# A new order of the image step in a vision transformer layer with routed experts

## The chip, the cores and the metric

The kernel runs on one core of a Trainium2 chip. The metric is the time of one execution on the device in microseconds (us). "Before" was timed three times; the profile is of one more execution.

## What is computed

The reference is one transformer layer over 16 images of 128 tokens and 256 channels, all in float32:

```python
h = tok(x)                                   # x: (16, 4, 128, 256); softmax over 4 groups, weighted sum
h = h + attn(layernorm(h))                   # 16 heads of 16, relative position bias, softmax over 128 keys
h = h + moe(layernorm(h))                    # 8 experts 256 -> 1024 -> 256, the best two of each token
```

`tok` weighs four groups per channel, with weights from a small two-layer network. `moe` keeps the two largest gates of a token and sums the two experts' outputs, weighted.

## The kernel before

The program is written by hand for each engine. Every engine works through its own list in order, and semaphores (`wait_ge`, `then_inc`) hold an instruction until another engine has finished.

**Image stage.** Each engine has a function `step(i, u, ...)`, called for i = 0 to 16. A step treats three images at a time, one pipeline stage apart: image i in front (`front`), i - 1 (`back`), i - 2 (`late`), with the preparation of i + 1 (`nxt`). What one step holds, by engine:

- TensorE (PE): `project_qk(i)` (L786) and `project_v(i)` (L797), 16 and 4 matmuls; `scores(i, 0)` and `scores(i, 1)` (L809), each for eight heads into the two banks `psS`, so that the second needs the first half's `biased` to be done; `context(i-1, c)` (L819), c = 0 to 3, transposes four heads' probabilities into `psP`; `values(i-1, w)` (L833) multiplies them with the values; `out_project(i-2)` (L844); `spread_sums`, `turn_x(i+1)` (L767), `turn_xn2(i-2)` (L859) are transposes; `gate_logits(i-2)` (L865); in steps 7, 11 and 14 also `ranks`.
- ScalarE (ACT): `exp(b, u, c)` (L592), four heads each, with row sums; `qk_evac` (L573), `pT_evac` (L581), `r_evac` (L567), `x1T_evac` (L561), `x2T_evac` (L609) and `v_evac` (L602) copy results of PE out of PSUM; `first_group(i+2)` (L553) starts the token mixing of a later image.
- VectorE (DVE): `select_groups(i+1)` (L1106) ends the token mixing, with the statistics of the first norm; `mask_keys(i, 0)` (L267); `residual(i-2)` (L1155), which waits for `project_v(i)` since both use the bank `psVO`, with the statistics of the second norm; `reciprocals` (L1136) and `spread` (L1140); `first_norm`, `second_norm` (L1093); `biased(i, c)` (L1126), c = 0 to 3, adds the position bias to four heads' scores and finds the minimum that `exp(i, u, c)` needs; `normalise` (L1149); `keep_logits` (L1167). In gate steps (6, 10, 13) also the gates of a batch of images, and in rank steps (7, 11, 14) `rows` (L1219 to L1226), which turns ranks into record positions.
- GpSimd (POOL): the power -1/2 of both norms (L434), `mask_keys(i, 1)`, and `scatter_records` (L445), an indirect DMA for each image and choice. From the second pair on, a pair waits for the landing of the pair before (`scat`). Batch 2 (images 8 to 10) goes out as two pairs in step 14 and one in step 15.
- SyncE (SP) issues the plain DMAs in order: in each step the stores of `xn2` and `h`, in every second step a load of 1 MB of W2 (L318), then, behind the tile table that DVE makes after step 14 (L1302 to L1323), the first load of W1 (L330), and behind the landing of all records of images 0 to 10 the records' reload (L323, L336).

**Expert stage.** 39 tiles of 128 token slots; each is gathered from DRAM (L482), transposed (L935), multiplied with W1 (L947) and W2 (L959), and scattered with addition (L491). The first 14 tiles use only images 0 to 10.

Of the kernel before, what the change touches and what calls it, by code (L numbers as in the profile page):

```python
# [63 lines left out]
def vit_layer_kernel(nc, x, tok_w1, tok_b1, tok_w2, tok_b2, Wq, Wk, Wv, Wo, rel_emb,  # L64
# [8 lines left out]
    with ExitStack() as ctx:  # L73
# [442 lines left out]
        def _(act):  # L516
# [39 lines left out]
            def x1T_evac(b):  # L556

                act.wait_ge(x1T_ps, b + 1)
                if later(b):
                    act.wait_ge(v_ps, b)  # L560
                act.copy(x1T[:, :], psQK[:, DC * S:2 * DC * S]).then_inc(x1T_sb, 1)  # L561
# [13 lines left out]
            def pT_evac(b, c):  # L575
                act.wait_ge(pT_ps, NCH * b + c + 1)
                if isinstance(b, int) and b == 0 and c < 2:
                    pass
                else:
                    act.wait_ge(pv_ps, NCH * b + c - 1)  # L580
                act.copy(pT[c % 2][:, :], psP[c % 2][:, :]).then_inc(pT_sb, 1)  # L581

            def exp(b, u, c):
                act.wait_ge(s_min, NCH * b + c + 1)
                if c == 0 and later(b, 1):
                    act.wait_ge(s_rcp, b - 1)
                own_wait(act)
                for n in range(CH):
                    h = c * CH + n
                    k = HEADS * (u % 2) + h  # L590
                    blk = prob[u % 2][:, h * S:(h + 1) * S]
                    i = act.activation(blk, blk, ACT.Exp, bias=smin[:, k:k + 1], scale=-1.0,  # L592
                                       accum_out=ssum[:, k:k + 1])
                i.then_inc(s_exp, 1)
# [14 lines left out]
                act.copy(x2T[:, :], psG[:, 0:DC * S]).then_inc(x2T_sb, 1)  # L609

            def step(i, u, front=True, back=True, late=True, nxt=True, batch=None, tanh=False, ahead=True):
                if back:
                    exp(i - 1, 1 - u, 2)
                if front:
                    qk_evac(i)
                if back:
                    pT_evac(i - 1, 0)
                    pT_evac(i - 1, 1)
                    exp(i - 1, 1 - u, 3)
                if tanh:  # L620
                    select_tanh(1, NG - 1)
                if batch is not None:
                    gate_exps(batch)
                if back:
                    pT_evac(i - 1, 2)
                    pT_evac(i - 1, 3)
                if back:
                    r_evac(i - 1)
                if ahead:
                    first_group(i + 2)  # L630
                if front:
                    exp(i, u, 0)
                if late:
                    x2T_evac(i - 2)
                if nxt:
                    x1T_evac(i + 1)
                if front:
                    exp(i, u, 1)
                    v_evac(i)

            def gate_exps(g):
                act.wait_ge(gate_exp_in, g + 1)
                n = BATCHES[g][1]
                act.activation(second_e[:, 0:n], below[:, 0:n], ACT.Exp).then_inc(gate_exp, 1)
# [59 lines left out]
        def _(pe):  # L704
# [8 lines left out]
            for g in range(G):  # L713
                i = pe.transpose(psVO[:, g * P:(g + 1) * P], tok_w2_wide[:, g * P:(g + 1) * P], ident[:, :])
# [56 lines left out]
            def spread_sums(b):  # L771

                pe.wait_ge(s_wide, b + 1)
                for c in range(DC):
                    i = pe.transpose(psCX[:, (DC + c) * S:(DC + c + 1) * S],
                                     srcw[:, c * P:(c + 1) * P], ident[:, :])
                i.then_inc(r_ps, 1)
# [91 lines left out]
            def ranks(g, last):  # L869

                pe.wait_ge(gate_step, GATE_N * g + MASKS_AT)
                pe.wait_ge(lg_sb, last)
                n = BATCHES[g][1]
                pe.matmul(psG[:, RKC:RKC + (n + 1) * E], ones[:, :], counts[:, 0:(n + 1) * E], start=True, stop=False)
                for k in range(1, n + 1):
                    pe.matmul(psG[:, RKC + k * E:RKC + (n + 1) * E], ones[:, :], counts[:, 0:(n + 1 - k) * E],
                              start=False, stop=False)
                pe.matmul(psG[:, RKC:RKC + n * E], before[:, :], counts[:, E:(n + 1) * E],
                          start=False, stop=True).then_inc(rank_ps, 1)

            def step(i, u, front=True, back=True, late=True, nxt=True, batch=None, sums=False, select=False):

                if front:
                    project_qk(i)
                if back:
                    context(i - 1, 1 - u, 0)
                    context(i - 1, 1 - u, 1)
                if late:
                    out_project(i - 2)
                if front:  # L890
                    project_v(i)
                if sums:
                    image_sums(2, 1)
                if batch is not None:
                    ranks(batch, i - 2)
                if back:
                    values(i - 1, 0)
                    context(i - 1, 1 - u, 2)
                if front:
                    scores(i, 0)  # L900
                if back:
                    context(i - 1, 1 - u, 3)
                    spread_sums(i - 1)
                if late:
                    turn_xn2(i - 2, batch)
                if nxt:
                    turn_x(i + 1)
                if back:
                    values(i - 1, 1)
                if front:  # L910
                    scores(i, 1)
                if select:
                    pe.wait_ge(x2T_sb, i - 1)
                    select_logits(1, NG, B)
                if late:
                    gate_logits(i - 2)
# [85 lines left out]
        def _(dve):  # L1002
# [93 lines left out]
            def select_groups(b, done=None):  # L1096

                dve.wait_ge(tok_first, b + 1)
                for g in range(1, G):
                    if g == 2 and done is not None:  # L1100
                        top_two(*done)
                    if g == 3 and done is not None:
                        top_index(*done)
                    if g > 1:
                        dve.wait_ge(tok_acc, (G - 1) * b + g - 1)
                    dve.scalar_tensor_tensor(out=hcol(b), in0=xw2[:, bass.ds(b * (G * D) + g * D, D)],  # L1106
                                             scalar=tsel[:, bass.ds(b + g * B, 1)], in1=hcol(b),
                                             op0=ALU.mult, op1=ALU.add).then_inc(tok_acc, 1)
                dve.wait_ge(tok_acc, (G - 1) * (b + 1))
                norm_stats(0, hcol(b), ln1, LN1_N * b)  # L1110

# [116 lines left out]
            def step(i, u, front=True, back=True, late=True, nxt=True, done=None, gate=None, place=None, hidden=False):  # L1228

                if nxt:  # L1230
                    select_groups(i + 1, done)
                elif done is not None:
                    top_two(*done)
                    top_index(*done)
                if gate is not None:
                    gate_inputs(gate)
                if front:
                    mask_keys(dve, i, 0)
                if late:
                    residual(i - 2)  # L1240
                if back:
                    reciprocals(i - 1, 1 - u)
                    spread(i - 1)
                if nxt:
                    first_norm(i + 1)
                if place is not None:
                    rows(place)
                if late:
                    second_norm(i - 2)
                if gate is not None:  # L1250
                    masks(gate)
                if front:
                    biased(i, u, 0)
                    biased(i, u, 1)
                if hidden:
                    hidden_end(1, NG - 1)
                if gate is not None:
                    gates(gate)
                if back:
                    normalise(i - 1)  # L1260
                if front:
                    biased(i, u, 2)
                    biased(i, u, 3)
                if late:
                    keep_logits(i - 2)

            hidden_start(0, 1)
            hidden_end(0, 1)
            select_weights(0, 0, NG)
            select_groups(0)  # L1270
            first_norm(0)
            bias_rows()
            step(0, 0, back=False, late=False)
# [144 lines left out]
```

## Time and profile before

| | us |
|---|---|
| median of 3 runs | 532.65 (532.6 to 533.27) |
| profiled execution, its own time | 531.54 |
| its span, first to last instruction | 529.5 |
| image stage, up to the first expert transpose | 223.12 |
| granted clock of TensorE, mean | 0.979 |

Times in the rows are counted from the span's start. In a window's row stand its bounds, its length, then the busy time of PE, PE's weight loads, DVE, ACT and POOL (instructions in brackets), the granted clock of TensorE, the DMA engines' share and GB/s. In a timeline's row stand start, length, engine, line, operation, output and inputs; the brackets at its end are the engine's idle time just before and what ended it. In the chain of waits the rows are pieces of the one chain that ended last. A row of ACT with one of four `exp` instructions stands for the start of its group. SPq is SyncE's queue.

Step 8 is the step that begins with `project_qk(8)` at 121.18 in the chain (121.04 in the timeline).

### The profile page before, as it was taken

The numbers are of one execution on the slowest core, as the hardware profiler recorded it, in microseconds if no ns is written. First come the engines' busy times: TensorE is split into PE (matmuls) and PEld (weight loads), VectorE is DVE, ScalarE is ACT, GpSimd is POOL, SyncE is SP. The second block draws the span as 40 slices with busy tenths as digits, with TensorE's granted clock in tenths as the row PEclk, the third lists the DMA queues.
The fourth block names the chain that finished last, engine by engine and source line by source line (L and its number), as shares of the span: only waits on it lengthen the run. The fifth ranks groups of instructions, "written<-read, shape, count | busy, mean of one in ns | idle before, by whom it ended". The sixth has DMA issues, their size and how long they took to land.

```text
span 529.5 us, 13085 instructions
## 1 busy us (share of the span) xinstructions
PE 480.4 (91%) x3742; PEld 408.0 (77%) x3743; DVE 219.0 (41%) x1068; ACT 261.7 (49%) x1003; POOL 178.2 (34%) x186
## 2 busy tenths in 40 slices
PE   3779989999999998699999999999999999999970
PEld 2457756676767675499999899999999999999960
DVE  2575788887888887422331111111111111111110
ACT  1247799889998888734323322233322333222310
POOL 3011123223334633313266533333332333333321
PEclk9889999999999999989999999999999999999995
DMA  8792030313213036287576556666667666677415
GB/s 269 220 351 72 22 101 22 102 40 102 77 46 101 22 103 183 60 295 191 181 196 158 161 183 196 193 162 164 184 194 198 178 161 171 184 197 187 123 20 168
DMA packets 51004, 78.61 MB, mean 148 GB/s; under 512 B 10528, under 2 KB 39472, under 8 KB 50768
## 3 DMA queue, kind: packets, MB, share of 16 engines
q1 hardware_dynamic: 40160, 66.80, 39.1%
q0 software_dynamic: 8592, 10.58, 11.8%
q10 hardware_dynamic: 2208, 0.71, 0.6%
q8 instruction: 20, 0.33, 0.3%
q14 instruction: 24, 0.20, 0.2%
HBM read 68.27 MB, written 11.90 MB: 151 GB/s over the span
## 4 chain that ended last, share of the span: by engine, by line
PE 71%; issue 10%; DVE 7%; ACT 5%; DMA 3%; POOL 3%; POOLq 0%; DVEq 0%; SPq 0%; ACTq 0%
PE psVO L959 24%; PE psS L947 13%; PE psP L947 13%; PE psQK L786 4%; PE psP L819 4%; PE psS L809 3%; ACT prob L592 3%; DVE prob L1126 2%; PE psVO L797 2%; PE psVO L844 2%; PE psQK L935 2%; DMA fold<-xn_dram,sel 1%; PE psG L865 1%; PE psCX L833 1%; POOL meta_dram L445 1%
## 5 line engine op out<-in xcount | busy, mean ns | idle before, releaser
L959 PE MATMUL psVO<-xw,prob 128*128 x624 | 141.7, 380 | 0.8 <-DVE fold L1348 0.8
L959 PEld LDWEIGHTS psVO<-xw,prob 128*128 128x128 f32 x624 | 115.5, 190 | 15.7 <-issue 1.2
L491 POOL DMA_INDIRECT sum_dram<-fold,sel x39 | 62.0, 1590 | 163.4 <-DMA sel<-meta_dram 112.3
L592 ACT ACTIVATE prob<-prob,smin 128x128 f32<-128x128 f32 x256 | 99.9, 400 | 4.7 <-DVE smin L1126 4.4
L679 ACT ACTIVATE prob<-psS,b1T 128x128 f32<-128x128 f32 x160 | 45.6, 368 | 94.3 <-PE psS L947 94.3
L679 ACT ACTIVATE prob<-psP,b1T 128x128 f32<-128x128 f32 x152 | 43.3, 368 | 92.5 <-PE psP L947 92.5
L947 PEld LDWEIGHTS psS<-fold,w1c 128*128 128x128 f32 x640 | 76.0, 195 | 1.7 <-DVE fold L1343 0.9
L947 PE MATMUL psS<-fold,w1c 128*128 128x128 f32 x640 | 76.5, 279 | 0.6 <-DVE fold L1343 0.6
L947 PEld LDWEIGHTS psP<-fold,w1c 128*128 128x128 f32 x608 | 70.8, 192 | 0.9
L947 PE MATMUL psP<-fold,w1c 128*128 128x128 f32 x608 | 71.0, 275 | 0.0
L434 POOL TENSOR_TENSOR rstd<-ve,minus_half 128x1 f32<-128x1 f32 x32 | 23.8, 743 | 135.2 <-DVE ve L1089 133.3
L1348 DVE TENSOR_TENSOR fold<-psVO,relb 128x256 f32<-128x256 f32 x39 | 16.6, 425 | 122.1 <-PE psVO L959 122.1
L1126 DVE CUSTOM_DVE_ANT_0 prob<-psS,relb 128x128 f32<-128x128 f32 x256 | 56.7, 286 | 18.5 <-PE psS L809 18.2
L1343 DVE COPY fold<-psQK 128x256 f32<-128x256 f32 x39 | 16.6, 425 | 107.0 <-PE psQK L935 107.0
L592 ACT ACTIVATION_READ_ACCUMULATOR prob<-prob,smin 128x1 f32 x256 | 50.7, 198 | 0.0
L581 ACT COPY pT<-psP 128x512 f32<-128x512 f32 x64 | 35.8, 588 | 20.6 <-PE psP L819 20.6
L482 POOL DMA_INDIRECT fold<-xn_dram,sel x39 | 38.9, 998 | 15.6 <-issue 11.7
L809 PE MATMUL psS<-kbd,qkT 64*128 64x512 f32 x128 | 37.0, 652 | 6.2 <-DVE smin L1126 5.0
L819 PEld LDWEIGHTS psP<-ident,prob 128*128 128x128 f32 x256 | 28.0, 141 | 15.7 <-ACT prob L592 8.9
L445 POOL DMA_INDIRECT meta_dram<-meta,pos x32 | 31.9, 998 | 23.5 <-DMA meta_dram<-meta,pos 10.8
L819 PE MATMUL psP<-ident,prob 128*128 128x128 f32 x256 | 37.9, 280 | 0.7 <-ACT prob L592 0.7
L786 PE MATMUL psQK<-x1T,wT 128*128 128x128 f32 x256 | 32.6, 280 | 0.5 <-ACT x1T L561 0.5
(166 smaller groups left out, 490.0 us busy)
## 6 DMA issues: line engine op xcount, KB each, us to landing
w1c<-in_L_ffn_W SPq DMA_DIRECT2D x39, 1024.0 KB
xw<-in_x SPq DMA_DIRECT2D x16, 512.0 KB, 7.8
xw<-in_L_ffn_W SPq DMA_DIRECT2D x8, 1024.0 KB, 6.5
sum_dram<-h_all SPq DMA_DIRECT2D x17, 128.0 KB
xn_dram<-xn SPq DMA_DIRECT2D x16, 128.0 KB, 1.7
out<-sum_dram SPq DMA_DIRECT2D x4, 512.0 KB, 5.7
relb<-in_L_ffn_b SPq DMA_DIRECT2D x1, 1024.0 KB, 7.9
sel<-meta_dram SPq DMA_DIRECT2D x39, 2.0 KB
```

Source lines behind the costliest of these rows:

```text
L445: pool.indirect_dma_start(out=meta_dram.ap()[:, :], out_offset=bass.IndirectOffsetOnAxis(ap=pos[:, i:i + 1], axis=0), in_=meta[:, i * META ...
L482: pool.indirect_dma_start(out=xs[j % 2], out_offset=None, in_=xn_dram.ap()[0:EARLY_B * S if j < EARLY else N_TOK, :], in_offset=bass.Indir ...
L491: pool.indirect_dma_start(out=sum_dram.ap()[0:EARLY_B * S if j < EARLY else N_TOK + P, :], out_offset=bass.IndirectOffsetOnAxis(ap=row_no[ ...
L581: act.copy(pT[c % 2][:, :], psP[c % 2][:, :]).then_inc(pT_sb, 1)
L592: i = act.activation(blk, blk, ACT.Exp, bias=smin[:, k:k + 1], scale=-1.0, accum_out=ssum[:, k:k + 1])
L679: i = act.activation(hT[u][:, c * P:(c + 1) * P], hidden_ps[u][c // 4][:, c % 4 * P:(c % 4 + 1) * P], ACT.Gelu, bias=b1T[:, bass.ds(e * HC ...
L786: i = pe.matmul(psQK[:, (t * DC + oc) * S:(t * DC + oc + 1) * S], wT[t][:, ic * D + oc * P:ic * D + oc * P + P], x1T[:, ic * S:(ic + 1) * ...
L809: pe.matmul(psS[r][:, :], qkT[rows, w * S:(w + 1) * S], kbd[rows, w * CH * S:(w + 1) * CH * S], start=True, stop=True).then_inc(s_ps, 1)
L819: i = pe.transpose(psP[c % 2][:, n * S:(n + 1) * S], pr[:, h * S:(h + 1) * S], ident[:, :])
L947: i = pe.matmul(hidden_ps[u][c // 4][:, c % 4 * P:(c % 4 + 1) * P], w1c[u][:, d * H + c * P:d * H + (c + 1) * P], xsT[:, d * P:(d + 1) * P ...
L959: i = pe.matmul(psVO[:, 0:D], hT[u][:, c * P:(c + 1) * P], xw2[:, bass.ds(e * (HC * D) + c * D, D)], start=(c == 0), stop=(c == HC - 1))
L1126: i = dve.tensor_tensor_reduce(prob[u % 2][:, h * S:(h + 1) * S], psS[c % 2][:, n * S:(n + 1) * S], relb[:, h * S:(h + 1) * S], 1.0, HIGHE ...
```

## The change

Only the order inside the steps changes, on three engines. `norm_stats` is taken out of `select_groups` into a function of its own, `first_stats`, so that it can stand elsewhere.

- ACT: `qk_evac(i)` goes ahead of `exp(i-1, 2)`. `exp(i, 0)` goes ahead of `pT_evac(i-1, 2)`. `x1T_evac(i+1)` goes ahead of `x2T_evac(i-2)`.
- PE: `scores(i, 0)` comes right behind `project_v(i)` (and `ranks`), ahead of `values(i-1, 0)` and `context(i-1, 2)`. `scores(i, 1)` comes ahead of the turns and of `values(i-1, 1)`. `turn_x` comes ahead of `turn_xn2`.
- DVE: `mask_keys(i, 0)` comes ahead of the first norm's statistics. `biased(i, 0)` comes behind `residual(i-2)`, ahead of the reciprocals; `biased(i, 1)` behind them, ahead of both norms. `second_norm` comes ahead of `rows`, and `rows`, `masks` and `gates` come behind the first two quarters of `biased`. `normalise(i-1)` comes last but one.

```diff
--- before.py
+++ after.py
@@ -609,11 +609,10 @@
                 act.copy(x2T[:, :], psG[:, 0:DC * S]).then_inc(x2T_sb, 1)
 
             def step(i, u, front=True, back=True, late=True, nxt=True, batch=None, tanh=False, ahead=True):
-                if back:
-                    exp(i - 1, 1 - u, 2)
                 if front:
                     qk_evac(i)
                 if back:
+                    exp(i - 1, 1 - u, 2)
                     pT_evac(i - 1, 0)
                     pT_evac(i - 1, 1)
                     exp(i - 1, 1 - u, 3)
@@ -621,19 +620,18 @@
                     select_tanh(1, NG - 1)
                 if batch is not None:
                     gate_exps(batch)
+                if front:
+                    exp(i, u, 0)
                 if back:
                     pT_evac(i - 1, 2)
                     pT_evac(i - 1, 3)
-                if back:
                     r_evac(i - 1)
                 if ahead:
                     first_group(i + 2)
-                if front:
-                    exp(i, u, 0)
+                if nxt:
+                    x1T_evac(i + 1)
                 if late:
                     x2T_evac(i - 2)
-                if nxt:
-                    x1T_evac(i + 1)
                 if front:
                     exp(i, u, 1)
                     v_evac(i)
@@ -893,22 +891,21 @@
                     image_sums(2, 1)
                 if batch is not None:
                     ranks(batch, i - 2)
+                if front:
+                    scores(i, 0)
                 if back:
                     values(i - 1, 0)
                     context(i - 1, 1 - u, 2)
-                if front:
-                    scores(i, 0)
-                if back:
                     context(i - 1, 1 - u, 3)
                     spread_sums(i - 1)
+                if front:
+                    scores(i, 1)
+                if nxt:
+                    turn_x(i + 1)
                 if late:
                     turn_xn2(i - 2, batch)
-                if nxt:
-                    turn_x(i + 1)
                 if back:
                     values(i - 1, 1)
-                if front:
-                    scores(i, 1)
                 if select:
                     pe.wait_ge(x2T_sb, i - 1)
                     select_logits(1, NG, B)
@@ -1106,6 +1103,9 @@
                     dve.scalar_tensor_tensor(out=hcol(b), in0=xw2[:, bass.ds(b * (G * D) + g * D, D)],
                                              scalar=tsel[:, bass.ds(b + g * B, 1)], in1=hcol(b),
                                              op0=ALU.mult, op1=ALU.add).then_inc(tok_acc, 1)
+
+            def first_stats(b):
+
                 dve.wait_ge(tok_acc, (G - 1) * (b + 1))
                 norm_stats(0, hcol(b), ln1, LN1_N * b)
 
@@ -1236,31 +1236,34 @@
                     gate_inputs(gate)
                 if front:
                     mask_keys(dve, i, 0)
+                if nxt:
+                    first_stats(i + 1)
                 if late:
                     residual(i - 2)
+                if front:
+                    biased(i, u, 0)
                 if back:
                     reciprocals(i - 1, 1 - u)
                     spread(i - 1)
+                if front:
+                    biased(i, u, 1)
                 if nxt:
                     first_norm(i + 1)
+                if late:
+                    second_norm(i - 2)
                 if place is not None:
                     rows(place)
-                if late:
-                    second_norm(i - 2)
                 if gate is not None:
                     masks(gate)
-                if front:
-                    biased(i, u, 0)
-                    biased(i, u, 1)
                 if hidden:
                     hidden_end(1, NG - 1)
                 if gate is not None:
                     gates(gate)
-                if back:
-                    normalise(i - 1)
                 if front:
                     biased(i, u, 2)
                     biased(i, u, 3)
+                if back:
+                    normalise(i - 1)
                 if late:
                     keep_logits(i - 2)
 
@@ -1268,6 +1271,7 @@
             hidden_end(0, 1)
             select_weights(0, 0, NG)
             select_groups(0)
+            first_stats(0)
             first_norm(0)
             bias_rows()
             step(0, 0, back=False, late=False)
```

## Rows read from the trace of the kernel before

**Rows 1.** Windows of steps 6, 7 and 8
```profile
97.44:108.88 11.44, 10.40 (x92) 7.44 (x92) 9.70 (x58) 10.34 (x45) 2.64 (x3) 1.00 0.30 103
108.88:121.18 12.30, 11.59 (x103) 8.91 (x104) 10.23 (x61) 10.23 (x43) 4.60 (x5) 1.00 0.19 36
121.18:132.34 11.16, 10.40 (x91) 7.45 (x92) 9.00 (x53) 10.12 (x43) 4.54 (x5) 1.00 0.33 105
```

**Rows 2.** Chain of waits, step 8: start, length, what
```profile
121.18 1.89 PE psQK L786 x16
...
126.95 1.06 PE psS L809 x4
...
131.73 0.61 PE psG L865 x4
132.34 0.66 PE psQK L786 x5
```

**Rows 3.** Timeline of ScalarE (ACT), step 8: start, length, [idle before it <-releaser]
```profile
124.03 0.58 ACT L573 COPY qkT<-psQK 128x512 f32<-128x512 f32 x1
124.50 1.07 ACT L581 COPY pT<-psP 128x512 f32<-128x512 f32 x2
125.45 0.42 ACT L592 ACTIVATE prob<-prob,smin 128x128 f32<-128x128 f32 x1
...
128.63 0.59 ACT L581 COPY pT<-psP 128x512 f32<-128x512 f32 x1 [1.04 <-PE psP L819]
...
129.79 0.40 ACT L592 ACTIVATE prob<-prob,smin 128x128 f32<-128x128 f32 x1
...
131.32 0.36 ACT L609 COPY x2T<-psG 128x256 f32<-128x256 f32 x1
131.58 0.37 ACT L561 COPY x1T<-psQK 128x256 f32<-128x256 f32 x1
```

**Rows 4.** Timeline of DVE and PE, step 8
```profile
125.78 0.42 DVE L1155 TENSOR_TENSOR h_all<-h_all,psVO 128x256 f32<-128x256 f32 x1 [0.43 <-PE psVO L797]
...
127.22 0.25 DVE L1136 RECIPROCAL srcp<-ssum 128x16 f32<-128x16 f32 x1
...
127.72 0.75 DVE L1093 TENSOR_SCALAR xn<-h_all,mv,rstd 128x256 f32<-128x256 f32 x2
...
130.31 1.13 PE L809 MATMUL psS<-kbd,qkT 64*128 64x512 f32 x4
...
131.63 0.29 DVE L1126 CUSTOM_DVE_ANT_0 prob<-psS,relb 128x128 f32<-128x128 f32 x1 [0.95 <-PE psS L809]
```

**Rows 5.** Timeline of DVE and ACT, step 15
```profile
209.32 0.28 DVE L1126 CUSTOM_DVE_ANT_0 prob<-psS,relb 128x128 f32<-128x128 f32 x1
...
210.38 0.40 ACT L592 ACTIVATE prob<-prob,smin 128x128 f32<-128x128 f32 x1 [0.72 <-DVE smin L1126]
...
211.00 0.42 DVE L1149 TENSOR_TENSOR ctxT<-psCX,rT 128x256 f32<-128x256 f32 x1
```

**Rows 6.** Timeline, from step 14 to the first expert tile
```profile
195.13 0.64 PE L833 MATMUL psCX<-pT,v_s 128*32 128x128 f32 x16
...
196.54 0.20 DVE L1219 TENSOR_TENSOR at_row<-psG,hot 128x48 f32<-128x48 f32 x1
...
198.50 0.45 SPq L318 DMA_DIRECT2D xw<-in_L_ffn_W  x1
...
204.97 0.95 POOL L445 DMA_INDIRECT meta_dram<-meta,pos  x1 [4.55 <-DMA meta_dram<-meta,pos]
...
206.34 0.40 SPq L330 DMA_DIRECT2D w1c<-in_L_ffn_W  x1
...
213.22 1.03 POOL L445 DMA_INDIRECT meta_dram<-meta,pos  x1 [4.37 <-DMA meta_dram<-meta,pos]
...
223.12 0.41 PE L935 MATMUL psQK<-ident,fold 128*128 128x128 f32 x2 [2.13 <-DMA fold<-xn_dram,sel]
```

**Rows 7.** Issues of DMAs, 198 to 206 us; last: us to landing
```profile
xw<-in_L_ffn_W SPq DMA_DIRECT2D x1, 1024.0 KB, 6.0
```

## The prediction

> **What bounds the kernel now.** Times are in us. I began with the share of the chain by line. The expert stage, from 223.12 on, is an unbroken run of matmuls which the diff doesn't touch; its beginning is a gather that the matrix engine (PE) waits 2.13 for, and I count everything behind it as moving with it [rows 6]. So the question is when that gather can come.
>
> Next the windows, one image step each. An ordinary step takes 11.16, one with gate work 11.44, one with a rank computation 12.30; ScalarE (ACT) is busy for 10.12 of the 11.16 [rows 1]. The chain of waits shows the loop of the ordinary step: from one `project_qk` (121.18) to the next (132.34), over the scores at 126.95 and `gate_logits` at 131.73 [rows 2]. ACT's timeline shows the one stall: `pT_evac(3)` sits 1.04 for the fourth transposed group, because PE did the next image's scores first [rows 3]. That stall is on the loop.
>
> Last, the end of the image stage. GpSimd (POOL) scatters the third batch's records in three pairs; each pair waits until the pair before has landed (4.55 and 4.37 idle), and behind the third pair come the records' reload and the first gather [rows 6]. From `rows(2)` at 196.54 to the first expert transpose at 223.12 are 26.58, on POOL and the DMA engines alone. PE finishes its own work 2.13 earlier. So the expert stage begins when `rows(2)` on VectorE (DVE) says, plus the landings.
>
> **The change in the ordinary step.** No instruction is added or removed, only `first_stats` is split off; all is order. I add up the new loop, `project_qk`'s start on the chain being 0.
> - DVE reaches `residual(i-2)`, which waits for `project_v(i)`, at 125.78 - 121.18 = 4.60 [rows 2, 4]. Scores are now right behind `project_v`. DVE needs 127.22 - 125.78 = 1.44 for residual and statistics [rows 4]. So `biased(i,0)` may begin at 6.04. The scores do not hold it: they begin with the end of `project_v` too, at about 4.60, and 1.32 from scores to biased (130.31 to 131.63 [rows 3, 4]) gives 5.92.
> - From a biased quarter's start to the exponential that waits for it, 210.38 - 209.32 = 1.06 [rows 5]. `exp(i,0)` starts at 7.10.
> - Could ACT take it earlier? `qk_evac` now starts with the end of `project_qk`, 1.89 and a few hundredths [rows 2], 1.92; then the copy 0.47, `exp(i-1,2)` 1.53, two copies 0.95, `exp(i-1,3)` 1.53 [rows 3]: 6.40. So ACT stands for 0.70, a new wait for DVE.
> - Then `exp(i,0)` 1.53, `pT_evac(2)` 0.48, and `pT_evac(3)`, `r_evac` and `first_group` 129.79 - 128.63 = 1.16; now `x1T_evac` 0.26, and only then `x2T_evac`, 131.73 - 131.32 = 0.41 to `gate_logits`, 0.61 to the next `project_qk` [rows 2, 3]. Sum 7.10 + 1.53 + 0.48 + 1.16 + 0.26 + 0.41 + 0.61 = **11.55**.
>
> The 1.04 on `pT_evac(3)` is gone, since the transposes finish while ACT is in `exp(i,0)`; but 0.70 comes back in front of `exp(i,0)`, `pT_evac(2)` (0.48) is now on the loop, and `x2T_evac` stands behind `x1T_evac` (0.26). 11.16 - 1.04 + 0.70 + 0.48 + 0.26 = 11.56: **0.39 slower**. ACT pays it as a wait for `project_qk` ahead of `qk_evac`, some 0.7.
>
> Gate steps: the gate's DVE work now lies behind the first two biased quarters and off the loop, so 11.55 in place of 11.44 here; I take +0.15 for each of three. Rank steps: the ranks' 1.14 (12.30 - 11.16) now lie ahead of the scores: 5.92 + 1.14 = 7.06 against 6.04 for the residual, 1.02 more, 12.57, +0.3 each, twice. Ordinary steps 4, 5, 8, 9, 12: 5 x 0.39 = 1.95. Steps 1 to 3 have other work in them (image sums, selection); bounds are 0 and twice the loop's loss, I take 0.39 each, 1.17. Up to step 14: 1.95 + 0.45 + 0.6 + 1.17 = **+4.2**.
>
> **The change in step 14.** `rows(2)` moves behind both biased quarters and `second_norm`. Before it began 1.41 after the slot behind the ranks (195.13 to 196.54 [rows 6]). Now scores take the slot: 1.32 to biased, 0.85 a quarter (eight blocks 211.00 - 209.32 = 1.68, halved [rows 5]), reciprocal and spread 127.72 - 127.22 = 0.50, another 0.85, two norms about 0.35 each (0.75 for both with the last one's tail [rows 4]): 4.2. **+2.8.** Queued behind it on DVE: quarters 2 and 3, which need the second scores at about the same moment (cost nothing), and on POOL the record pairs, with `mask_keys(15,1)` and so `scores(15,1)` behind the second pair.
>
> **What the landings give back.** The first pair is issued just before the last W2 load (198.50). The load lands 6.0 after its issue [rows 7], at 204.5; the next pair goes out at 204.97. The second pair is followed by the first W1 load (206.34), and its landing comes only at 213.22 [rows 6]. Both slow pairs have a load of 1 MB beside them, so I read the wait as the load's. The W2 load follows `second_norm(12)`, which now precedes `rows(2)`: against `rows(2)` it comes 1.0 earlier (a norm 0.35, and `rows` itself, four small instructions of which the first has 0.20, an estimated 0.65). The W1 load follows the tile table, which stood behind `second_norm`, two quarters and the wait for second scores: 9.80 - 0.35 - 1.70 - 0.95 = 6.8 behind `rows(2)` [rows 4 to 6]. It landed, by the pair, 6.9 after its issue: 13.7 in place of 16.68. **-3.0** in all (the 1.0 is within it). Bounds: 0, if the pairs take a time of their own, and -5.4, if pair one lands 1.0 earlier and nothing is left of the 4.37 before pair three.
> The Trainium skill (DMA: Bandwidth & Descriptors, Queues, rings and completion order) says that a completion's count is written only after all earlier writes of the same DMA engine, whatever queue they came by. The trace agrees so far: 204.97 is 0.47 behind the load. By it the full -3.0 comes; by a landing of fixed length, nothing.
>
> PE's own end moves too: +4.2 and about 0.4 for the like of it in step 14. Less its 2.13 of slack it would ask for +2.5 at the first gather, and stays behind the sum below.
>
> **Sum.** 4.2 + 2.8 - 3.0 = +4.0. The profiled execution took 531.54 (span 529.5 and 2.0 around it); the median of the runs is 532.65, 1.1 above it. 531.54 + 4.0 = 535.5, so on the median 532.65 + 4.0 = **536.7**.
>
> **Rivals.**
> - *The landings move with the pairs.* +7.0: 539.7. For it: the pairs' 4.55 and 4.37 are nearly equal though the loads stand differently to them. Against it: both ends follow a load.
> - *DVE is not late (the other side).* Place: `exp(i,0)` behind `biased(i,0)`. If biased is through 0.70 earlier than summed (by a residual that isn't held by `project_v`, or scores that overlap), ACT's own loop decides: 11.55 - 0.70 = 10.85, 0.31 faster in eight steps and 0.59 in the three gate steps, -4.3; with 2.8 - 3.0 it is -4.5, 528.2. It decides from 0.4 on (11.16). Against it: 4.60 + 1.44 are measured, only the order is new.
> - *The stall goes and nothing takes its place.* ScalarE's 10.12 sets the step: 1.04 in each of some ten steps, -10.4, 522. For it: rows 3 show this stall alone on ACT. Against it: `exp(i,0)` gains a producer that isn't ready.
> The Trainium skill (Trace Analysis, Identifying the Most-Contended Engine) has the engine with the highest occupancy optimized first. By that rule ScalarE with 10.12 of 11.16 is the one, and taking its only gap away is the right edit; the sum shows two other gaps opening.
> - *Neutral:* steps' loss half as large, landings a bit better than thought: within 0.2%.
>
> **Numbers.** Forecast 0.45; landings move along 0.23; DVE not late 0.10; stall simply gone 0.03; neutral 0.11; more than 540.7 0.08. About 0.2% (1.1) is what a measurement of this kernel can tell from nothing. Slower are the first two, the last and 0.02 of neutral: 0.78; same 0.09; faster 0.13. The range goes from 533.8 (half the steps' loss, 2.1 + 2.8 - 3.0, is 534.6; another 0.8 of the landings' further 2.4) to 540.7 (no gain from the landings and 0.1 more in ten steps).
>
> **What would show it.** Ordinary steps of 11.5 to 11.6; ACT without idle before `pT_evac(3)`, but idle before `exp(i,0)` (from DVE, about 0.7) and before `qk_evac` (from PE, about 0.7); `rows(2)` near 203.5; the gap from there to the first expert transpose near 23.6 in place of 26.58; the expert stage as long as before. Wrong if the step is below 11.3, or if the gap stays.

## The result, and the profile after

| | before | after |
|---|---|---|
| median of 4 runs | 532.62 (530.03 to 533.27) | 537.75 (536.52 to 538.26) |
| profiled execution | 531.54 | 537.61 |
| its span | 529.5 | 535.6 |

The recorded ratio is 1.0111 [1.0078, 1.0145], slower; the two medians alone are 5.1 apart, which would be 1.0096. The forecast was 536.7 in [533.8, 540.7], with 0.78 on slower.

Windows of steps 7, 8 and 9 after the change, columns as in [rows 1]:

```profile
111.11:123.72 12.61, 11.75 (x104) 8.91 (x104) 9.88 (x59) 10.23 (x45) 3.10 (x4) 1.00 0.07 21
123.72:135.49 11.77, 10.60 (x92) 7.39 (x92) 9.08 (x53) 10.23 (x45) 5.45 (x7) 1.00 0.41 115
135.49:147.26 11.77, 10.60 (x92) 7.39 (x92) 9.06 (x53) 10.22 (x45) 4.14 (x5) 1.00 0.08 24
```

In step 8, PE, DVE and ACT are each busy to within 0.2 of [rows 1] (in step 7 DVE is busy 0.35 less), but the ordinary step is 0.61 longer. ScalarE's timeline of step 8, as [rows 3]:

```profile
125.64 0.59 ACT L573 COPY qkT<-psQK 128x512 f32<-128x512 f32 x1 [0.79 <-PE psQK L784]
...
128.62 0.41 ACT L592 ACTIVATE prob<-prob,smin 128x128 f32<-128x128 f32 x1
...
131.02 0.40 ACT L592 ACTIVATE prob<-prob,smin 128x128 f32<-128x128 f32 x1 [0.75 <-DVE smin L1126]
...
132.57 1.04 ACT L581 COPY pT<-psP 128x512 f32<-128x512 f32 x2
133.51 0.37 ACT L567 COPY rT<-psCX 128x256 f32<-128x256 f32 x1
133.78 0.52 ACT L553 ACTIVATE h_all<-xw,tsel 128x256 f32<-128x256 f32 x1
134.19 0.36 ACT L561 COPY x1T<-psQK 128x256 f32<-128x256 f32 x1
134.44 0.39 ACT L609 COPY x2T<-psG 128x256 f32<-128x256 f32 x1
```

The 1.04 ahead of `pT_evac(3)` is gone: the two copies at 132.57 run back to back. In its place stand the two waits that the forecast named, 0.75 for DVE ahead of `exp(i,0)` (131.02) and 0.79 for `project_qk` ahead of `qk_evac` (125.64). The chain of waits in the same step shows why DVE is late:

```profile
127.35 0.88 PE psVO L795 x4
...
128.32 0.43 DVE h_all L1155
...
128.89 0.44 DVE st L1081
...
129.68 0.04 DVE ve L1086
129.72 0.05 issue
129.77 0.05 DVEq L275
129.82 0.13 issue
129.95 0.29 DVE prob L1126
```

`residual` starts with the end of `project_v`, 128.32 - 123.72 = 4.60 behind `project_qk` on the chain, as forecast; `biased(i,0)` starts 1.63 later, at 129.95, where 1.44 was forecast. Between the last statistics and it lie 0.23 of queue time.

Now the starts of the steps, read as the starts of `project_qk` in PE's timeline, and from them how much longer each kind of step became:

| | before | after | longer | forecast |
|---|---|---|---|---|
| start of step 0 | 26.11 | 25.20 | -0.91 | none |
| steps 0 to 3 | 48.87 | 50.11 | 1.24 | 1.17 |
| ordinary, 4, 5, 8, 9, 12 | 55.80 | 58.84 | 3.04 | 1.95 |
| gate, 6, 10, 13 | 34.14 | 35.66 | 1.52 | 0.45 |
| rank, 7 and 11 | 24.62 | 25.22 | 0.60 | 0.6 |
| step 14 to `rows(2)` | 7.00 | 9.81 | 2.81 | 2.8 |
| `rows(2)` to first expert transpose | 26.58 | 24.59 | -1.99 | -3.0 |
| first expert transpose | 223.12 | 229.43 | 6.31 | 4.0 |

The expert stage behind it is as long as before (306.4 and 306.2). POOL's timeline after, from `rows(2)` (204.84) on, shows the landings:

```profile
206.39 1.04 POOL L445 DMA_INDIRECT meta_dram<-meta,pos  x1 [4.47 <-DVE pos L1226]
...
212.36 0.96 POOL L445 DMA_INDIRECT meta_dram<-meta,pos  x1 [3.65 <-DMA meta_dram<-meta,pos]
...
218.58 1.03 POOL L445 DMA_INDIRECT meta_dram<-meta,pos  x1 [2.35 <-DMA meta_dram<-meta,pos]
...
225.56 1.02 POOL L482 DMA_INDIRECT fold<-xn_dram,sel  x1 [0.29 <-issue]
```

SyncE's, with the two loads:

```profile
205.82 0.45 SPq L318 DMA_DIRECT2D xw<-in_L_ffn_W  x1
211.45 0.40 SPq L330 DMA_DIRECT2D w1c<-in_L_ffn_W  x1
```

The third pair goes out 13.74 behind `rows(2)` where it was 16.68 [rows 6]; W2 is loaded 0.98 behind it and W1 6.61. The forecast had 13.7, 0.96 (198.50 - 196.54 = 1.96 before, less 1.0) and 6.8. The other 0.95 of the forecast's 3.0 are lost behind the third pair: from there to the gather 6.98 in place of 6.78, from the gather to the transpose 3.87 in place of 3.12.

### The profile page after: what moved, and what is told of

The parts are those of the page before. It is cut to its first block, busy times and chain, and to the rows that moved or that the text cites. A ratio compares the mean times of both kernels' runs of the same rounds, so it can differ in the third digit from the quotient of the medians.

```text
span 535.6 us, 13085 instructions
## 1 busy us (share of the span) xinstructions
PE 485.3 (91%) x3742; PEld 408.9 (76%) x3743; DVE 217.7 (41%) x1068; ACT 262.1 (49%) x1003; POOL 171.6 (32%) x186
## 4 chain that ended last, share of the span: by engine, by line
PE 73%; DVE 8%; DMA 6%; issue 5%; ACT 4%; POOL 1%; POOLq 0%; DVEq 0%; ACTq 0%
PE psVO L956 23%; PE psS L944 12%; PE psP L944 12%; PE psQK L784 5%; PE psS L807 4%; DVE prob L1126 4%; DMA fold<-xn_dram,sel 3%; PE psP L817 2%; PE psVO L795 2%; PE psVO L842 2%; PE psQK L932 2%; ACT prob L592 2%; PE psG L863 2%; PE psCX L831 1%; DMA kbd<-rel_dram 1%
## 5 line engine op out<-in xcount | busy, mean ns | idle before, releaser
L1126 DVE CUSTOM_DVE_ANT_0 prob<-psS,relb 128x128 f32<-128x128 f32 x256 | 57.8, 287 | 19.2 <-PE psS L807 17.1
L434 POOL TENSOR_TENSOR rstd<-ve,minus_half 128x1 f32<-128x1 f32 x32 | 17.8, 556 | 143.7 <-DVE ve L1086 139.9
L592 ACT ACTIVATION_READ_ACCUMULATOR prob<-prob,smin 128x1 f32 x256 | 49.5, 193 | 0.0
L817 PE MATMUL psP<-ident,prob 128*128 128x128 f32 x256 | 35.9, 279 | 0.4 <-ACT prob L592 0.2
L581 ACT COPY pT<-psP 128x512 f32<-128x512 f32 x64 | 33.5, 571 | 0.3 <-PE psP L817 0.3
```

The source lines that it names most:

```text
L817: i = pe.transpose(psP[c % 2][:, n * S:(n + 1) * S], pr[:, h * S:(h + 1) * S], ident[:, :])
L1126: i = dve.tensor_tensor_reduce(prob[u % 2][:, h * S:(h + 1) * S], psS[c % 2][:, n * S:(n + 1) * S], relb[:, h * S:(h + 1) * S], 1.0, HIGHE ...
```

## Experiments

All ratios are to the kernel before on the same chip. Step lengths are those of undisturbed ordinary steps in the profiled execution.

**a_turn_order**, after with the turns and their copies back in the old order.

```diff
-                if nxt:
-                    x1T_evac(i + 1)
                 if late:
                     x2T_evac(i - 2)
+                if nxt:
+                    x1T_evac(i + 1)
...
-                if nxt:
-                    turn_x(i + 1)
                 if late:
                     turn_xn2(i - 2, batch)
+                if nxt:
+                    turn_x(i + 1)
```

> The changed kernel with one part undone: ScalarE copies x2T ahead of x1T again, and TensorE turns xn2 ahead of x again. My theory: in the changed kernel the loop of a step runs over ScalarE (exp(i,0), two pT copies, r, first group, x1T, x2T, gate_logits, project_qk), so the copy of x1T (0.26) drops out of it: the step goes from 11.77 to 11.5, and twelve such steps give about -2.5 to -3, near 535. Rival: TensorE's own path over biased(i,1), the second scores, the turns and values(i-1,1) sets the step, 0.2 behind; then the step stays above 11.6 and the time within 1 us of 537.75.

1.0058 [1.0024, 1.0091]; ordinary step 11.49 to 11.50, 0.27 shorter. The 0.26 for `x1T_evac` ahead of `x2T_evac` are a term of the loop, as summed.

**a_exp_late**, after with `exp(i,0)` back behind the copies.

```diff
-                if front:
-                    exp(i, u, 0)
                 if back:
                     pT_evac(i - 1, 2)
                     pT_evac(i - 1, 3)
                     r_evac(i - 1)
                 if ahead:
                     first_group(i + 2)
+                if front:
+                    exp(i, u, 0)
```

> The changed kernel with the part undone that names the change: ScalarE does exp(i,0) behind the last two pT copies, r_evac and first_group again; all else as changed. My theory, worked out from the measured pieces: the copies then wait for the transposes and the row-sum transposes, which stand behind the first scores on TensorE and behind biased(i,0) on VectorE, and exp(i,0) is ready at 9.0 after project_qk instead of 7.4: step 11.7, no more than 0.1 from the changed kernel's 11.77, time 537 to 538. Rival: the early exp(i,0), which waits 0.75 for VectorE, is itself the cost; undoing it gives back the 0.61 of every ordinary step, 11.2, near 532.6.

1.0102 [1.0071, 1.0134]; step 11.68. Putting `exp(i,0)` early costs 0.09 a step here. With it undone and all else kept the kernel stays slow, as expected, so the loss isn't made by that move alone.

**a_rows_early**, after with `rows` right behind `residual`.

```diff
                     residual(i - 2)
+                if place is not None:
+                    rows(place)
...
                     second_norm(i - 2)
-                if place is not None:
-                    rows(place)
```

> The changed kernel with rows() of the rank steps right behind residual, ahead of biased(i,0). rows(2) then starts near 201.3 instead of 204.84. Theory of the loads: the record pairs wait for a landing only where a load of 1 MB is under way; the W2 and W1 loads stay where they are (205.8 and 211.5), so the second pair leaves near 207 and the third when VectorE and POOL have done step 15's second norm, 214 to 216. Theory of fixed landings: the pairs keep their distances of 5.97 and 6.22, second pair near 208.8, third near 215. In both the first gather comes 3 to 4 earlier, and TensorE, whose own work in the image stage ends at 228.6 in the changed kernel, 0.8 ahead of the gather, takes over as the bound: gain only 0.5 to 1.5, 536.5 to 537.3.

1.0066 [1.0034, 1.0098]; steps 11.77, `rows(2)` 6.18 behind the step's start in place of 9.81. POOL's timeline of it:

```profile
202.94 1.04 POOL L445 DMA_INDIRECT meta_dram<-meta,pos  x1 [0.81 <-DVE pos L1226]
...
206.67 0.96 POOL L445 DMA_INDIRECT meta_dram<-meta,pos  x1 [1.41 <-DMA meta_dram<-meta,pos]
...
214.59 1.03 POOL L445 DMA_INDIRECT meta_dram<-meta,pos  x1 [0.21 <-issue]
```

The W2 load goes out at 206.00 here, 3.06 behind the first pair, and the second pair goes 3.73 behind the first. In after the load preceded the pair and the distance was 5.97 (206.39 to 212.36). A landing of fixed length is refuted. From the start of step 14 to the first expert transpose it is 32.04 in place of 34.40, so the gain is 2.4, more than was expected of it. PE did take over as the bound (it does not idle before that transpose), but its own end also came 1.5 earlier, 32.06 behind the start of step 14 in place of 33.57.

**b_w1_late**, before with the first W1 load behind the records' reload.

```diff
             sp.wait_ge(tables_ok, 1)
-            load_w1(0, 0)
             store_xn2(B - 3)
...
             load_records(0)
+            load_w1(0, 0)
```

> The kernel before with one change: SyncE issues the first W1 load only behind the landing of all record pairs and the reload of the first records, instead of beside the second pair. Theory of the loads: the second pair lands without a load beside it, some 2 behind its issue, and the third leaves near 209.5 instead of 213.22; the gather comes 3 to 4 earlier, TensorE's own end (221.0, against 223.12 for the gather) takes over: -1 to -2, 530.7 to 531.6. Theory of fixed landings: the third pair still leaves near 213.2, and the time stays or gets longer, since W1 comes later.

0.9976 [0.9949, 1.0003]: 1.7 faster by the medians, as expected, but the interval reaches past 1. POOL's timeline of it:

```profile
203.42 0.96 POOL L445 DMA_INDIRECT meta_dram<-meta,pos  x1 [4.61 <-DMA meta_dram<-meta,pos]
204.68 0.96 POOL L445 DMA_INDIRECT meta_dram<-meta,pos  x1 [0.30 <-issue]
...
208.03 1.03 POOL L445 DMA_INDIRECT meta_dram<-meta,pos  x1 [0.74 <-DVE xn L1093]
```

The first pair still has the W2 load beside it and its 4.61. Behind the second pair the idle time is 0.74 in place of 4.37 [rows 6]: the third goes out 13.09 behind `rows(2)` (194.94), before it was 16.68. Of these 3.6 the first expert transpose keeps 1.85 (24.73 in place of 26.58 behind `rows(2)`); PE's own end, 0.24 before that transpose, would have allowed hardly more. The load, at 213.60, now stands between the records' reload (212.47) and the first gather (216.39), and the two are 3.92 apart where they were 2.60; whether the load makes that difference was not tested.

**a_waits_ahead**, after with two waits of `biased(i,0)`, both met long before, moved ahead of `mask_keys`.

```diff
             def biased(b, u, c):
-                if c == 0 and not (isinstance(b, int) and b <= 1):
-                    dve.wait_ge(pT_ps, NCH * (b - 1))
-                if c == 0 and not (isinstance(b, int) and b <= 1):
-                    dve.wait_ge(s_exp, NCH * (b - 1))
...
                 if front:
+                    if i > 1:
+                        dve.wait_ge(pT_ps, NCH * (i - 1))
+                        dve.wait_ge(s_exp, NCH * (i - 1))
                     mask_keys(dve, i, 0)
```

> The changed kernel, but the two waits of biased(i,0) on work of image i-2 (transposes done, exponentials done), which are met long before, stand ahead of mask_keys(i,0) instead of in front of biased(i,0). Theory: of the 0.19 by which biased(i,0) starts later behind the residual than forecast (1.63 instead of 1.44), some 0.05 each is VectorE's queue working through waits that are already met; step 11.77 to about 11.67, -1 in all, within what the timing can tell. Rival: the 0.19 is the pipeline between two instructions; the step stays 11.77.

1.008 [1.0053, 1.0108]; step 11.66 to 11.67. A wait that is already met costs DVE's queue 0.05, and on this loop that is a term.

**b_fill_stall**, before with two moves on ACT: `first_group` into its one stall, and `x2T_evac` ahead of `exp(i,0)`.

```diff
+                if ahead:
+                    first_group(i + 2)
                 if back:
                     pT_evac(i - 1, 2)
...
                 if back:
                     r_evac(i - 1)
-                if ahead:
-                    first_group(i + 2)
+                if late:
+                    x2T_evac(i - 2)
                 if front:
                     exp(i, u, 0)
-                if late:
-                    x2T_evac(i - 2)
```

> The kernel before with two moves on ScalarE only: first_group(i+2) ahead of pT_evac(2), into the stall of 1.04 before pT_evac(3), and x2T_evac(i-2) ahead of exp(i,0). Theory: the stall is filled with 0.41 of work that is needed anyway, and gate_logits no longer waits for the end of exp(i,0); ordinary step 11.16 to 10.9, step 14 begins 2 to 3 earlier, and the record pairs with it: -2 to -3, near 529.5. Rival: TensorE's order of first scores and last transposes sets the step whatever ScalarE does; 11.1 and no gain.

0.9939 [0.9918, 0.996]; step 10.80. Its ACT timeline in step 8:

```profile
125.66 0.51 ACT L553 ACTIVATE h_all<-xw,tsel 128x256 f32<-128x256 f32 x1
126.06 0.58 ACT L581 COPY pT<-psP 128x512 f32<-128x512 f32 x1
127.28 0.59 ACT L581 COPY pT<-psP 128x512 f32<-128x512 f32 x1 [0.64 <-PE psP L819]
```

The idle time before `pT_evac(3)` falls from 1.04 to 0.64 by the 0.40 of `first_group`, and the step by 0.36. PE's timeline shows where the 0.36 lies, first before, then here:

```profile
131.73 0.61 PE L865 MATMUL psG<-wg_s,x2T 128*128 128x8 f32 x4 [0.30 <-ACT x2T L609]
```

```profile
128.87 1.13 PE L809 MATMUL psS<-kbd,qkT 64*128 64x512 f32 x4
129.93 0.61 PE L865 MATMUL psG<-wg_s,x2T 128*128 128x8 f32 x4
```

From `scores(i,1)` to `gate_logits` it was 1.42 (130.31 [rows 4] to 131.73) and is 1.06: PE no longer waits for `x2T_evac`. So work behind the stall on ACT was on the loop, as read. But `first_group` out of the way (0.41) and `x2T_evac` ahead of `exp(i,0)` (1.53) would each, by these rows, have covered that wait of 0.30, which is an estimate; no run has one without the other.

**b_all**, b_fill_stall with three more: PE's `values(i-1,0)` behind `scores(i,0)`; on DVE `rows` and `first_norm` right behind `residual`; `masks` behind `biased(i,1)` (on DVE only the new places are shown).

```diff
-                    values(i - 1, 0)
                     context(i - 1, 1 - u, 2)
...
                 if back:
+                    values(i - 1, 0)
                     context(i - 1, 1 - u, 3)
...
                     residual(i - 2)
+                if place is not None:
+                    rows(place)
+                if nxt:
+                    first_norm(i + 1)
...
                     biased(i, u, 1)
+                if gate is not None:
+                    masks(gate)
```

> b_fill_stall, and on TensorE values(i-1,0) behind scores(i,0) instead of ahead of context(i-1,2), and on VectorE rows() right behind residual, first_norm ahead of the reciprocals, masks() behind biased(i,1). Theory: transposes and first scores come 0.6 earlier, gate work leaves the loop: ordinary step 10.9, gate steps 11.1 instead of 11.4, rank steps 11.7 instead of 12.3, rows(2) 5 earlier than before; the record pairs still wait beside both loads: -4 to -5, near 528. Rival: below 11 per step another order binds (VectorE before the first biased quarter), and the sum is that of b_fill_stall.

0.997 [0.9944, 0.9996], 0.7 by the medians where 4 to 5 was expected. Ordinary steps are 11.04, 0.24 worse than with the ACT edit alone; only gate steps (11.02, 11.13 in place of 11.48, 11.41) and rank steps (11.63 for 11.82) gain. **b_all_w1** is the same with the late W1 load.

> b_all together with the late first W1 load of b_w1_late. Theory: both gains add up, since one moves TensorE's end of the image stage and rows(2), the other the last record pair: the first expert transpose comes when TensorE is through, 6 earlier than before, -5 to -6.5, near 526.5. Rival: the W1 load, now issued behind the records' reload, lands after the first gather and holds hidden(0): the gain of b_all and no more.

0.9939 [0.9919, 0.996]; the first expert transpose comes 26.63 behind `rows(2)`, with 28.38 in b_all. By the medians it is 3.4 faster than before, where 5 to 6.5 was expected. Which of PE's and DVE's edits costs the 0.24 isn't taken apart; the next kernels leave the moves of `values` and `first_norm` out.

**f_fill_w1** is b_fill_stall with the late W1 load.

> b_fill_stall with the late first W1 load of b_w1_late. b_fill_stall's profile has ordinary steps of 10.80, but TensorE sits idle for 2.61 ahead of the first expert transpose and then runs its first tile at a granted clock that has fallen. Theory: the late load lets the third pair go 3 earlier and closes most of this gap: ratio near 0.990, -5 to -6 (the two kernels alone had 0.9939 and 0.9976). Rival: records' reload and first gather, now beside the W1 load, lose what the pair gains, as in b_all_w1: 0.993 to 0.994.

0.9942 [0.9915, 0.9968]: not the 0.990 of the theory but its rival's 0.993 to 0.994, so the late W1 load adds nothing that the timing shows to b_fill_stall's 0.9939. **f_fill_w1_gate** is that with `rows` behind `residual` and `masks` behind `biased(i,1)`, without the moves of `values` and `first_norm`.

> f_fill_w1 and on VectorE rows() right behind residual and masks() behind biased(i,1). Theory: of b_all's moves those on TensorE made the ordinary step 11.04 instead of 10.80, those on VectorE made the gate steps 11.02 to 11.14 instead of 11.4; so here ordinary steps 10.8, gate steps 11.1, rows(2) 0.8 earlier in its step: another -1 to -2 against f_fill_w1. Rival: TensorE's end of the image stage bounds, and rows() ahead of the reciprocals delays it: no change.

0.9916 [0.9882, 0.9949], median 528.36 where before has 532.33: faster than both kernels. Its windows of step 8:

```profile
118.22:129.01 10.79, 10.33 (x92) 7.45 (x92) 9.06 (x53) 10.15 (x45) 4.54 (x5) 1.00 0.36 116
```

Gate steps are 10.97, 10.89 and 10.93, where f_fill_w1 has 11.48, 11.41 and 11.41. The medians of the two (528.36, 528.61) can't be told apart. The gate steps give 1.5, but from the start of step 14 to the first expert transpose it is 34.57 in place of 31.83. The first pair now goes out 1.22 before the W2 load (192.18 and 193.40), the second pair waits 6.26 for the first one's landing (4.55 in f_fill_w1), and `mask_keys(15,1)` stands behind it on POOL. Beside that DVE's copy `srcw` took 1.50, the granted clock fell to 0.50, and `scores(15,1)` took 2.08 in place of 1.13; PE's own end came 33.46 behind the start of step 14 in place of 31.17. This is read from the two traces, not tested. In a_rows_early and a_three, where `rows` is early too but the W2 load leaves 3.0 and more behind the first pair, the second pair waited 1.4 and PE's own end came at 32.06 and 31.73.

**a_three** is after with a_turn_order, a_waits_ahead and a_rows_early together.

> The changed kernel with the three edits together that were tried one by one on it: turns and copies in their old order (-0.28 a step), the met waits ahead (-0.10), rows() right behind residual (-3.4 for rows(2)). Theory: the ScalarE loop shortens by both, 11.4 per ordinary step, rows(2) near 196.5 as in the kernel before; TensorE's own end bounds, some 3 later than before: ratio 1.002 to 1.005. Rival: once ScalarE's loop is shorter, TensorE's path over the second scores takes over at 11.5, ratio 1.005 to 1.007.

0.9998 [0.9967, 1.0028]; steps 11.39 to 11.40 (11.77 - 0.27 - 0.10 = 11.40), `rows(2)` 6.17 into its step. Three small edits give the whole loss back, as far as the timing tells. The steps don't account for all of it: they stay 0.24 above before's 11.16, and no run takes that rest apart; the first expert transpose comes 197.97 behind the start of step 0, where it is 197.01 in before.

## Why the forecast held, and where its sum was off

**The mechanism was right.** The stall went, two waits came, `rows(2)` moved by 2.81 against 2.8. The rivals: *the stall goes and nothing takes its place* and *DVE is not late* fall with ACT's 0.75 at 131.02. *The landings move with the pairs* falls with b_w1_late, a_rows_early and the -2.94 up to the third pair. The neutral one, *steps' loss half as large*, falls with 0.61. What the runs attribute of the ordinary step's 0.61 is 0.27 to the order of the turns and their copies and 0.10 to the met waits; `exp(i,0)` put back gains 0.09 by itself, and the 0.24 that a_three leaves stays unexplained.

**The mis-sized term is the steps' loss: +4.2 forecast, +6.40 measured.** It splits in two.
- Ordinary steps: 0.61 in place of 0.39, 1.1 over five. The term "1.44 for residual and statistics" measured 1.63, since in the trace of before `reciprocals` followed there and now `biased(i,0)` does, with more waits ahead of it; a_waits_ahead shows 0.10 of these 0.19. The other 0.09, and the 0.03 by which `x2T_evac` to `gate_logits` took 0.44 for 0.41, are only read, not tested.
- Gate steps: 1.52 in place of 0.45. The forecast took +0.15 for each, from 11.55 against 11.44. That the gate's work leaves the loop was right: steps 10 and 13 became ordinary steps of 11.77. Of the 1.07 too little, about 0.54 is the ordinary step's own error once more (11.77 is 0.18 above 11.44 + 0.15, three times), 0.17 that steps 10 and 13 were 11.36 and 11.35 before, not 11.44, and 0.35 that step 6 took 12.12. There DVE idles for 0.46 before `biased(6,0)`, with ACT as the releaser, and ACT for 1.00 before `exp(6,0)` in place of 0.75. Why, no run was made to tell.

**The landings: -3.0 forecast, -1.99 measured.** Up to the third pair they are right to 0.06. What fell short is behind it: the forecast let the gather follow the third pair, and the first transpose the gather, at the distances of before, and gave these two no term of their own. The gather in the chain of waits, before and then after:

```profile
217.40 1.71 DMA sel<-meta_dram
...
220.00 2.87 DMA fold<-xn_dram,sel
```

```profile
225.56 3.62 DMA fold<-xn_dram,sel
```

The gather is the same transfer. From its issue to the first transpose the 13 traces of this case show 3.02 to 3.87, and after has the longest; the 0.75 may therefore be chance, and no run settles it.

**The start.** Step 0 begins anywhere from 23.62 to 26.60 in the 13 traces, while the loads of the setup land. Before and after, at 26.11 and 25.20, differ by 0.91 for no cause in the diff. So errors partly cancel: 6.40 + 2.81 - 1.99 - 0.91 = 6.31 at the first transpose, 5.1 between the medians, 4.0 forecast. The 0.91 is luck in the forecast's favour: without it the first transpose would come 7.2 later.

**PE's own end** was put at +4.6, of which 2.5 past its slack. It moved by 7.6 (the last `gate_logits` ends at 228.6, where it was 221.0), and the slack of 2.13 fell to 0.83. Of the 3.0 too little in the forecast, 2.2 are the steps' (6.40 for 4.2) and 1.7 the stretch behind the start of step 14 (33.57 for 31.45, with 0.4 forecast; what happens there in step 15 is told below), less the start's 0.9.

## What to carry to other kernels

Before an instruction is moved into a stall, find when its input is ready: here `exp(i,0)` was put ahead of two copies and then waited 0.75 for its own input, while `first_group` and `x2T_evac`, whose inputs were there, together took 0.36 off each step. Sum the whole loop in its new order, with the waits that stand ahead of an instruction in its queue, and for each kind of step from its own row rather than from one of its kind.

A load of 1 MB holds up small transfers that others wait for, so its place is behind them; but look for the next bound before counting on the gain. Putting the W1 load there brought the third pair 3.6 forward, yet only 1.85 reached the first expert transpose. In time it gave 0.9939 for 0.997 in b_all, 0.9976 with an interval past 1 alone, and nothing in f_fill_w1.

## What the runs showed that was not expected

**A small transfer waits for a large one beside it.** From the end of the second pair's issues to the third pair's start it is 2.39 in b_w1_late (205.64 to 208.03), with no load beside it and other work last on POOL and DVE, and 6.03 in before, where the W1 load had gone out at 206.34, beside the pair. The trace agrees with the completion order that the Trainium skill gives (DMA: Bandwidth & Descriptors, Queues, rings and completion order). A small transfer that merely queues behind the load's data would look the same; no run tells the two apart.

**A DVE copy took three times its length beside a POOL operation.** In step 15 of after, DVE's timeline:

```profile
214.81 1.00 DVE L1140 COPY srcw<-srcp 128x256 f32<-128x256 f32 x1
```

and POOL's:

```profile
214.60 1.05 POOL L267 TENSOR_TENSOR kbd<-qkT,pmask 128x512 f32<-128x512 f32 x1
```

In step 8 the same copy takes 0.29 (131.08). The Trainium skill (GPSIMD Engine Reference, Specifications) says that POOL shares its interfaces to SBUF with VectorE and that VectorE's instructions in a 2-port mode contend there. The copy ends at 215.81 and POOL's operation at 215.65, which agrees; in which mode the copy ran, no row shows. The other traces bear the pairing out: in the eight where the copy of step 15 overlaps this POOL operation by 0.24 or more it takes 0.40 to 1.50 (0.40 in b_w1_late with 0.24, 1.50 in f_fill_w1_gate with the whole 1.05), and in before, b_fill_stall and f_fill_w1, with 0.14 or less, it takes 0.29. In a_rows_early it took 0.53 beside a record pair's issue instead. PE waited 1.34 for this copy in after.

**TensorE's clock fell behind such a gap.** Windows of after, columns as in [rows 1]:

```profile
215.00:216.00 1.00, 0.13 (x1) 0.14 (x2) 1.00 (x4) 1.00 (x7) 1.00 (x2) 1.00 0.98 406
216.00:217.00 1.00, 0.51 (x4) 0.30 (x6) 0.98 (x9) 1.00 (x5) 0.23 (x1) 0.79 0.16 41
217.00:218.00 1.00, 1.00 (x4) 0.30 (x4) 0.00 (x0) 0.61 (x2) 0.00 (x0) 0.50 0.12 41
```

PE was busy for 0.13 and 0.51 of two microseconds, then the granted clock was 0.50, the level of 1.2 GHz, for three and back at 1.00 from 220. The scores there took 2.08 in place of 1.13. The same came behind the wait for the first gather. Windows of a_three, whose PE was busy for 0.44 and 0.39 of the two microseconds from 221:

```profile
222.00:223.00 1.00, 0.39 (x3) 0.24 (x2) 0.70 (x5) 0.00 (x0) 0.05 (x1) 0.78 0.88 328
223.00:224.00 1.00, 1.00 (x6) 1.00 (x7) 0.06 (x1) 0.00 (x0) 0.90 (x1) 0.50 1.04 356
```

Its first 32 matmuls took 5.36; in f_fill_w1, where the clock stayed at 1.00, they took 3.84, although PE was busy there for only 0.41 and 0.43 of the two microseconds from 218. So the busy share just before does not tell which way it goes, and these runs leave it open. Before and after both show the fall in their first expert tile (0.50 from 225 to 227 and from 231 to 233), and their expert stages are equally long (306.4 and 306.2). Of the 13 traces only a_rows_early, b_w1_late and f_fill_w1 keep 1.00 there.
